# Attention and LoRA block: the same work on the same engines, each engine's list in another order

## What is computed

```python
x = L0_attn_x                                   # (2, 1024, 512), fp32
x = x + attn(_layernorm(x), Wq, Wk, Wv, Wo, q_norm_w, k_norm_w)
x = x + ffn(_layernorm(x), A, B, Wr, br)

# attn: 32 query heads, 8 key/value heads, head size 128, causal, ALiBi
q = rmsnorm(x @ Wq.T); k = rmsnorm(x @ Wk.T); v = x @ Wv.T
p = softmax(q @ k.T / sqrt(128) + slope * rel)  # rel > 0 is masked
out = (p @ v) @ Wo.T
# ffn: eight LoRA experts of rank 16, all of them used
scores = 8 * softmax(x @ Wr.T + br)
out = 2 * einsum('bshr,hor,bsh->bso', x @ A, B, scores)
```

## Time and profile before

| | before |
|---|---|
| runs, us | 2189.63, 2194.16, 2194.26 |
| profiled execution: its time, us | 2194.96 |
| its span, first to last instruction, us | 2193.1 |
| mean granted TensorE clock in it | 0.995 of full |
| PE busy | 2135.6 us, 97% |
| VectorE (DVE), ScalarE (ACT), GpSimd (POOL) busy | 63%, 52%, 37% |
| HBM over the span | 53 GB/s |

### The profile page before, as it was taken

One profiled execution on the slowest core, in us unless ns is written; L12 is line 12 of the kernel. 1 busy time (PEld: TensorE's weight loads), 2 busy tenths in 40 slices (PEclk: granted clock), 3 DMA queues, 4 the chain that ended last, 5 costly groups with the idle time before them and its releaser, 6 DMA issues.

```text
span 2193.1 us, 33323 instructions
## 1 busy us (share of the span) xinstructions
PE 2135.6 (97%) x12220; PEld 1834.4 (84%) x12220; DVE 1373.7 (63%) x3431; ACT 1149.2 (52%) x3314; POOL 802.1 (37%) x872
## 2 busy tenths in 40 slices
PE   7999999999999999999999999999999999999997
PEld 6888888888888888888888888888888888888885
DVE  5656656566565666669766556565556656565686
ACT  3555555465554655545545455454545545455542
POOL 2433424244242433424424344342424424243341
PEclk9999999999999999999999999999999999999999
DMA  4212111121210212111121011101001111101100
GB/s 173 87 58 87 59 57 46 43 87 58 87 58 1 87 58 78 63 38 65 58 97 39 20 39 39 59 39 59 2 38 58 39 58 39 44 15 39 39 15 24
DMA packets 32129, 118.01 MB, mean 54 GB/s; under 512 B 4185, under 2 KB 4185, under 8 KB 23777
## 3 DMA queue, kind: packets, MB, share of 16 engines
q1 hardware_dynamic: 31536, 115.89, 14.1%
q10 hardware_dynamic: 432, 0.01, 0.0%
HBM read 69.75 MB, written 46.14 MB: 53 GB/s over the span
## 4 chain that ended last, share of the span: by engine, by line
PE 91%; DVE 4%; ACT 2%; issue 1%; POOL 1%; DMA 0%; ACTq 0%; POOLq 0%; DVEq 0%
PE s_ps L923 26%; PE o_ps L923 18%; PE y_ps L923 16%; PE turn_ps L990 15%; PE q_ps L923 15%; DVE kT_lo L803 1%; DVE pT_lo L801 1%; PE y_ps L1079 1%; DVE oT_lo L848 1%; ACT qn L641 0%; ACT kT_hi L627 0%; ACT oT_hi L660 0%; PE turn_ps L984 0%; ACT pT_hi L625 0%; DVE low_gated L896 0%
## 5 line engine op out<-in xcount | busy, mean ns | idle before, releaser
L717 POOL TENSOR_TENSOR probs<-probs,p_inv 128x896 f32<-128x896 f32 (+7 forms) x512 | 578.0, 1150 | 784.8 <-DVE p_inv L821 784.5
L632 ACT ACTIVATE probs<-probs,neg_max 128x896 f32<-128x896 f32 (+7 forms) x512 | 396.6, 777 | 295.5 <-DVE neg_max L814 293.4
L814 DVE CUSTOM_DVE_ANT_0 probs<-s_ps,rel 128x896 f32<-128x896 f32 (+7 forms) x512 | 382.9, 753 | 268.1 <-issue 266.9
L625 ACT ACTIVATE pT_hi<-turn_ps 128x512 fp32r<-128x512 f32 x576 | 332.0, 597 | 308.6 <-PE turn_ps L990 308.5
L801 DVE TENSOR_TENSOR pT_lo<-turn_ps,pT_hi 128x512 fp32r<-128x512 f32 x576 | 384.6, 685 | 139.9 <-ACT pT_hi L625 138.8
L990 PE MATMUL turn_ps<-ident,probs 128*128 128x128 f32 x2464 | 343.7, 273 | 4.3 <-DVE probs L837 2.5
L990 PEld LDWEIGHTS turn_ps<-ident,probs 128*128 128x128 f32 x2464 | 295.1, 141 | 54.0 <-issue 5.4
L923 PE MATMUL s_ps<-kT_hi,qT_hi 128*128 128x512 f32 (+3 forms) x768 | 278.7, 363 | 14.1 <-DVE kT_lo L803 12.5
L923 PE MATMUL s_ps<-kT_hi,qT_lo 128*128 128x512 f32 (+3 forms) x768 | 263.1, 343 | 0.0
L923 PE MATMUL s_ps<-kT_lo,qT_hi 128*128 128x512 f32 (+3 forms) x768 | 261.8, 341 | 0.0
L923 PE MATMUL o_ps<-pT_hi,v_hi 128*128 128x512 f32 x576 | 243.2, 422 | 1.8 <-DVE pT_lo L801 1.7
(11 more groups left out here) (105 smaller groups left out, 3621.1 us busy)
## 6 DMA issues: line engine op xcount, KB each, us to landing
wq_raw<-in_L_attn_Wq SPq DMA_DIRECT2D x8, 1024.0 KB, 5.6
wo_raw<-in_L_attn_Wo SPq DMA_DIRECT2D x8, 1024.0 KB, 6.0
wq_kept<-wqT_hi SPq DMA_DIRECT2D x8, 1024.0 KB, 5.0
wq_kept<-wqT_lo SPq DMA_DIRECT2D x8, 1024.0 KB, 7.2
wo_kept<-woT_hi SPq DMA_DIRECT2D x8, 1024.0 KB, 7.0
wo_kept<-woT_lo SPq DMA_DIRECT2D x8, 1024.0 KB, 9.1
wqT_hi<-wq_kept SPq DMA_DIRECT2D x8, 1024.0 KB, 4.8
wqT_lo<-wq_kept SPq DMA_DIRECT2D x8, 1024.0 KB, 6.9
```

The costliest lines, as they stand in the source:

```text
L625: nc.scalar.activation(target, bank, ACT.Copy).then_inc(sems["high"], 1)
L632: nc.scalar.activation(row, row, ACT.Exp, bias=neg_max[:, s % 2, h:h + 1], scale=-1.0, accum_out=p_sum[:, s % 2, h:h + 1]).then_inc(sems[" ...
L717: nc.gpsimd.tensor_tensor(row, row, p_inv[:, s % 2, h:h + 1].to_broadcast((P, L)), ALU.mult).then_inc(sems["normalise"], 1)
L814: nc.vector.tensor_tensor_reduce(out=probs[:, s % 2, h, 0:L], in0=s_ps[:, at_col:at_col + L], in1=rel[:, S - L:S], scale=-float(slopes[w % ...
```

## The change

All six strings are written anew: the same items (each name once per window, as before), in another order; no engine gets or loses an item. One thing is added, a wait of VectorE before the first `max` of a window, for its own `v_low`, since the new order no longer has a wait that implies it. Two lines each of two strings stand for all of them:

```diff
 PROLOGUE = (
-    "load_y.0 load_y.1 load_y.2 load_y.3 load_wkv.first load_y.4 load_wq.first x_stats.0 load_y.5 load_y.6 x_stats.1 "
...
+    "load_y.1 load_wq.first load_y.0 load_y.3 load_y.5 load_y.6 load_y.2 load_wkv.first x_stats.1 load_y.4 x_stats.0 "
...
 GROUP_A = (
-    "turn.wo.0 high.wo.0 turn.wo.1 norm_q.1 high.wo.1 scores.0.0 low.wo.0 scores.0.1 turn.wo.2 max.0.0 q.2.0 max.0.1 "
...
+    "turn.wo.0 scores.0.0 high.wo.0 scores.0.1 max.0.0 turn.wo.1 max.0.1 exp.0.0 turn.wo.2 norm_q.1 exp.0.1 "
...
@@ -807,6 +809,8 @@
                 L = (s + 1) * P
                 if w == 0 and s == 0 and h == 0:
                     dve.wait_ge(rel_ready, 1)
+                if s == 0 and h == 0:
+                    after(dve, "v_low", w)
                 after(dve, "scores", w, s, h)
```

## The result

The changed kernel takes 2171.84 us in the median of four runs (2169.62 to 2173.52), the kernel before 2194.21 beside it (2189.63 to 2194.3): ratio 0.9902, 95% interval 0.9885 to 0.992, so 22.4 us less. The forecast was 2177.3, in a range of 2165 to 2189.

What follows compares the result with a forecast made beforehand. The prediction took PE, with work under way for 97% of the span, as the bound, so only its waits could be won. Its terms summed to 16.9 us won: 2178.1 profiled, 2177.3 as median, range 2165 to 2189.

Steps and rivals of the forecast that it cites:

- Boundaries of batch 0: Seven window boundaries, w = 0 to 6 into the next: net 1.25 us won each, 8.8 in all.
- the 0.35 for `q.2.0`: Batch 0 boundaries: `norm_q.1` ready 2.25 us after `y.7` against 1.98 of PE work, so about 0.35 lost.
- the upper bound of the text: Batch 0 boundaries: 1.6 us won at each of seven, 11.2 in all, if `norm_q.1` is in time.
- Nothing won or lost here: Seven batch 1 boundaries: losses of 3.2 to 3.3 us each after, against 3.4 before; taken as 0, bounds ±5.6.
- batch 1 gains too: Rival: the VectorE queue walk is pessimistic and batch 1 boundaries win 1.5 us each, time 2167; chance 15%.
- The clock: Batch 1 boundaries: one of two half-clock stretches of 3.4 us goes, 1.7 us won.
- slower rival: Batch 1 boundaries lose time in four pieces, each bringing two half-clock stretches; about 2199 us; chance 6%.
- 1.2 lost: Window 8: waits at `turn.q.1` and `scores.0.2` cost 2.4 us where 1.2 was; bounds 0 and 3.
- 2.4 won: Window 15: about 4.5 us of LoRA waits go, less five delays of 0.3 to 0.4 at `values`; bounds −2 and 5.
- 1 won: The end, `y.7` then the last tile's chain: fewer PE items left in it, 1 us won; bounds −1 and 3.
- all but the last three tiles have 5 to 24 us: Windows 7 and 15: PE work between `turn.logits` and `turn.lora`, where 2.5 to 5.5 us stood before.
- The start: Prologue with window 0: first transpose at about 12.2, first scores at 44.8 not 45.6, 2 us won; bounds −4 and 5.

Runs made afterwards that it cites:

- `y.7` put back: Changed kernel with `y.7` returned ahead of `turn.k.0` and `add_y.7` ahead of `high.k.1` in GROUP_A and GROUP_B: 2225.89 us, ratio 1.015.
- the experiment: Changed kernel with SyncE's `store.5` and `load_y.5` moved from window 7's list to behind `back_wo` and `back_wkv` of window 8: 2168.12 us, ratio 0.9882.
- the old LAST: Changed kernel with the old LAST string (window 15) in place of the new one: 2171.66 us, ratio 0.9893.
- fastest kernel: Changed kernel with `store.5`, `load_y.5` late in window 8 and, in GROUP_B, `q.9.3` between `turn.k.1` and `y.7`, `square_q.9`, `inv_q.9` behind `high.k.1`: 2165.27 us.
- `y.7` alone: Kernel before with only `y.7` moved behind `turn.k.1` and `add_y.7` behind `low.k.1`, in both group strings: 2195.69 us, ratio 1.0006.
- GROUP_A alone: Kernel before with only the new GROUP_A string (windows 0 to 6) and the added wait of VectorE: 2180.5 us, ratio 0.9939.
- the new start alone: Kernel before with only the new PROLOGUE string and the added wait of VectorE: 2189.49 us, ratio 0.9981.

## Why the prediction was right, and where not

- **What bounds it: right.** PE has the same 12,220 instructions, and its recorded busy time fell only from 2135.6 to 2125.9; the gain is waits and half clock at the boundaries.
- **Boundaries of batch 0: right in mechanism, a term too small.** 1.25 was forecast, 1.7 measured (2.3 in window 6). The failed step is the 0.35 for `q.2.0`. That `norm_q.1` ends 2.25 behind `y.7` was right (2.2); but the 1.98 of PE work counts twelve transposes and only two of the four scores that stand ahead of `q.2.0`. With all four it is 2.57, and `norm_q.1` is in time: the upper bound of the text. The experiments on `y.7` bear the mechanism out: put back, it costs 2.0 a window; moved alone, it wins nothing, since the transposes of k then wait for `norm_k`. The prediction had not named that the gain also needs cover between `kv.3` and the transposes of k. Which of the other moves gives it, no run shows.
- **Boundaries of batch 1: the sum was wrong by 0.8 each.** "Nothing won or lost here" should have been 0.8 × 6. The walk through VectorE's queue found the right waits, but sized them 3.2 to 3.3 where 2.75 came. `y.7` was right (0.8 and 0.80); `turn.q.1` (0.5 and 0.19), `scores.0.3` (0.15 and 0), `scores.0.0` (0.1 and 0) and `scores.0.2` (0.8 and 0.71) were too long, `values.0.0` too short (0.8 and 1.05). The loss of before, 3.4, was right within 0.2. Half of the rival "batch 1 gains too" was true.
- **The clock: right.** Both half-clock stretches of batch 1 went, of which one was forecast; 3.1 us of the 7.9, at 1.55 each. Its slower rival, stretches brought by several short waits, did not come about. `y.7` put back has half clock at six of six boundaries, but behind waits of 3.5 us, so it does not test that rival.
- **Window 8: the failed step.** "1.2 lost" came from PE's and VectorE's lists alone. It is 4.7, of which the late `woT_lo` is 6 (by the experiment), so that without it the window would have won 1.2. SyncE's queue was read only for the first transfers. The stores' order, with the end of `add_f.5` beside it, was there to be read.
- **LoRA: half right in window 7, wrong in window 15.** In window 7 the waits for `low_gated` went from 2.3 to 0.4, but `neg_max` now has 0.7, and 1.3 were won of 2.8. In window 15 they went from 3.4 to 5.7 (`turn.lora.4`, `.6` and `.7` at 1.5, 2.2 and 2.0), and `turn.q.1` and `scores.1.2` wait 0.9 and 0.8 near its start. "2.4 won", and "1 won" for the end, were worth nothing by the medians; the old LAST takes the same time. Over the kernel the `low_gated` waits are 6.1 us, where the prediction had named near zero as a sign of being right. The step that failed is "all but the last three tiles have 5 to 24 us": it counts from `turn.logits` in PE's list, but `f_low.4` stands in VectorE's list directly ahead of its `turn.lora.4`, and it met `normalise` there, so that it took 1.61 us for a median of 0.29 (timeline, DVE, after; GpSimd is in `normalise` from 2131.66 to 2135.46):

```profile
2132.09 1.61 DVE L900 TENSOR_TENSOR low_gated<-f_logits,f_gates 128x128 f32<-128x128 f32 x1
```

- **The start: right in mechanism.** PE's first instruction was forecast at 12.2 and came at 11.97. The first scores came at 43.0 instead of 44.8, since the bound on Wk and Wv hardly bit (the weight loads of their transposes waited 0.4 us for them), and the half clock of window 0 was not in the sum. Alone the new start is worth 4.2 for the 2 forecast; part of the 5.9 between the two traces is the execution of before, as said there.
- **Transposes to matmuls: 0.6 lost** can't be told from zero: window 2 is 130.9 us of which PE is recorded busy all.

Added up on the profiled executions, with 1.7 of window 0 counted as its boundary: too little by 3.7 for batch 0 (12.5 for 8.8), 3.9 for the start (5.9 for 2), 6.2 for batch 1 with its clock (7.9 for 1.7) and 0.6 for the transposes; too much by 3.5 in window 8, 1.5 in window 7 and 4.8 in window 15 with the end. These are 24.2 us of errors, of which 4.6 remain because the rest cancel. That the total came within 5.5 us of the median is in good part luck. No run has the new BOUNDARY or FIRST_B alone.

## What to carry to other kernels

When every engine follows one list, a long matmul block is a cover that can be spent once: ask at which of the waits around it it hides most, and what else was hidden where it stood. When you set a deadline against an engine's work, list every item between the two points; two scores left out made a wait of nothing. Read the list of the DMA queue as carefully as that of the bound engine, and look for a store whose data comes late, ahead of loads that something needs soon. And don't take it that a chain of waits will even itself out: with the 0.8 at `y.7` gone, those behind it stayed as long as they were.

## What was not expected of the hardware

The price of a wait on TensorE is often more than its length, and it is not the same each time. Behind some waits the granted clock falls to 1.2 GHz of 2.4. These are the counts over all traces for the main waits between the first scores and `y.7` of window 15:

| wait, us | where | half clock behind it |
|---|---|---|
| pieces up to 1.0 | all kernels with new lists | one, 3.4 us, from 2023.4 (fastest kernel, behind 0.96 and 0.83) |
| 1.4 | `kT_lo`, batch 0, `y.7` put back | none of six |
| 1.5 | `q.2.0` in window 0, old start and old GROUP_A | one of three (50.0, before) |
| 1.6 | `y.7` alone, both batches | none of thirteen |
| 1.5 and 1.7 | `low_gated`, window 15, tile 4 | none of ten |
| 1.8 | `kT_lo`, six traces | eight of 24: seven of 3.4 us, one of 6.8 |
| 2.4 | `turn_ps` for `pT_lo`, window 15, old LAST | one of six, 3.4 us |
| 1.5, 1.9, 3.2 | `woT_lo`, three traces | none, 3.4 us, 6.8 us |
| 3.5, with 1.4 ahead of it | `y.7` put back, batch 1 | six of six: four of 6.8 us, two of 3.4 |

A stretch of 3.4 us cost 1.6 (window 9 against 10, before). Four windows with a wait of 3.5 us and 6.8 us of half clock are 7.0 us over those of the changed kernel, 0.9 of it at `y.7`. Length alone doesn't decide it, since 2.4 us mostly brought none. Where it falls also varies under the same lists: of the seven boundaries with 1.8 us, the first and the fifth have it before and with GROUP_A alone, the first and the fourth with the new start alone. At the end of the kernel half clock takes 6.4 us of the span before and 7.6 to 14.0 in the changed kernels. What decides it stays open, and so does how far the end could be brought down.
